# A planner of engine orders: TensorE priced by its recent columns, new overheads, less room at hand-overs

## What is computed

```python
x = x + 0.5 * ffn(layernorm(x))     # gate, up: 512 -> 1408 (ternary weights, scaled), silu(g) * u, down: 1408 -> 512
x = x + attn(layernorm(x))
x = x + 0.5 * ffn(layernorm(x))

def attn(x):                        # I = 1024 channels, N = 16 states, R = 128
    h, gate = split(x @ W_in.T)     # 512 -> 2 * 1024
    h = silu(causal_conv4(h) + conv_b)
    ts, B, C = split(h @ Wx.T, [128, 144]); each rms-normed
    delta = softplus(ts @ Wdt.T + dt_bias)
    # for each channel and each of 16 states, along the sequence:
    s = exp(delta * A) * s + delta * B * h
    y = sum_n s * C + D * h
    return (y * silu(gate)) @ Wout.T
```

## Time and profile before

| | before |
|---|---|
| median of 3 runs | 2842.37 us (2838.3 to 2843.48) |
| the profiled execution | 2835.58 us, span of its instructions 2833.8 us |
| PE busy | 2386.6 us, 84%, 12266 instructions |
| DVE busy | 2466.0 us, 87%, 3115 instructions |
| ACT busy | 1757.4 us, 62%, 2995 instructions |
| POOL busy | 2275.5 us, 80%, 1387 instructions |
| mean granted TensorE clock | 0.922 |
| DMA | 606.66 MB, 214 GB/s, 63.5% of the 16 engines' time |

### The profile page before, as it was taken

The page is one execution under the profiler, slowest core; times in us unless marked ns, Lnnn a source line. Parts: engine busy times, 40 slices in busy tenths (PEclk is TensorE's granted clock), DMA queues, the critical chain, the costliest instruction groups (busy, mean ns, idle before and its releaser), DMA issues. The chain is left out here.

```text
span 2833.8 us, 38163 instructions
## 1 busy us (share of the span) xinstructions
PE 2386.6 (84%) x12266; PEld 1933.5 (68%) x12266; DVE 2466.0 (87%) x3115; ACT 1757.4 (62%) x2995; POOL 2275.5 (80%) x1387
## 2 busy tenths in 40 slices
PE   6779789689577998889988999889988886599968
PEld 5657677577466776677766877677776764477756
DVE  5649997897998989899999999899989988999973
ACT  5465667767656666576657765577657666465531
POOL 2257769779976889789996999779996889889852
PEclk9889899899789999999999999999999997599979
DMA  8655645846666467955778366955778388366544
GB/s 268 225 191 167 238 160 178 297 131 230 205 214 235 127 211 265 310 172 172 248 267 314 129 216 237 322 202 166 235 266 283 121 287 289 101 206 188 183 165 141
DMA packets 293952, 606.66 MB, mean 214 GB/s; under 512 B 23024, under 2 KB 23792, under 8 KB 293744
## 3 DMA queue, kind: packets, MB, share of 16 engines
q1 hardware_dynamic: 293744, 604.13, 63.5%
HBM read 451.47 MB, written 152.57 MB: 213 GB/s over the span
## 5 line engine op out<-in xcount | busy, mean ns | idle before, releaser
L1930 POOL TENSOR_TENSOR sbuf<-dus,bring 128x1024 f32<-128x1024 f32 x512 | 1217.9, 2394 | 181.3 <-PE pt L1403 94.4
L1556 ACT ACTIVATE pa<-dls,cst 128x512 f32<-128x512 f32 x1024 | 691.8, 688 | 432.3 <-DVE sbuf L1730 415.8
L1403 PE MATMUL pt<-ident,sbuf 128*128 128x128 f32 x4096 | 645.0, 294 | 210.9 <-DVE sbuf L1730 84.1
L1403 PEld LDWEIGHTS pt<-ident,sbuf 128*128 128x128 f32 x4096 | 507.2, 150 | 367.4 <-DVE sbuf L1730 131.9
L1322 PE MATMUL pm<-xT,wring 128*128 128x512 f32 x2816 | 708.0, 399 | 16.1 <-DVE xT L1613 6.4
L1730 DVE TENSOR_TENSOR_SCAN sbuf<-pa,sbuf 128x512 f32<-128x512 f32 x512 | 610.0, 1211 | 64.6 <-ACT pa L1556 53.4
L1730 DVE TENSOR_TENSOR_SCAN sbuf<-pa,carry,sbuf 128x512 f32<-128x512 f32 x512 | 631.9, 1268 | 35.2 <-POOL sbuf L1930 23.1
L1334 PE MATMUL pm<-wring,act 128*128 128x512 f32 x2176 | 581.4, 410 | 25.1 <-DVE hd L1658 9.4
L1322 PEld LDWEIGHTS pm<-xT,wring 128*128 128x128 f32 x2816 | 516.6, 189 | 120.3 <-issue 18.4
L1741 DVE SCALAR_TENSOR_TENSOR acc<-pt,cT,acc 128x512 f32<-128x512 f32 x768 | 548.0, 739 | 51.6 <-PE pt L1403 49.9
L1334 PEld LDWEIGHTS pm<-wring,act 128*128 128x128 f32 x2176 | 401.6, 193 | 113.4 <-issue 14.4
(11 more groups left out here) (142 smaller groups left out, 2285.9 us busy)
## 6 DMA issues: line engine op xcount, KB each, us to landing
wring<-wsp SPq DMA_DIRECT2D x408, 512.0 KB, 4.5
bring<-b_d SPq DMA_DIRECT2D x256, 256.0 KB, 3.9
xn_d<-tb SPq DMA_DIRECT2D x24, 1024.0 KB, 9.1
xnb<-xn_d SPq DMA_DIRECT2D x19, 1024.0 KB, 7.3
x_d<-tb SPq DMA_DIRECT2D x16, 1024.0 KB, 6.1
u_d<-hd SPq DMA_DIRECT2D x64, 256.0 KB, 5.7
sg_d<-hd SPq DMA_DIRECT2D x64, 256.0 KB, 4.3
tb<-x_d SPq DMA_DIRECT2D x16, 1024.0 KB, 6.8
```

The costliest lines, as they stand in the source:

```text
L1403: ins = e.matmul(pt[u.pt[tt]][:, k * P:(k + 1) * P], sbuf[:, u.s3, k, tt * P:(tt + 1) * P], ident[:, :], is_transpose=True, start=True, st ...
L1556: e.activation(pa[k % 2][:, :], dls[:, k, :], ACT.Exp, scale=col(C_A + (4 * u.ig + k) * N + u.n)).then_inc(S.a_exp, 1)
L1930: e.tensor_tensor(sbuf[:, u.s3, h * m:(h + 1) * m, :], dus[:, h * m:(h + 1) * m, :], bring[:, u.s2:u.s2 + 1, :].broadcast_to([P, m, TC]), ...
```

## The change

Three things are changed, all in the planner. No instruction, tile, buffer or semaphore is added or removed; only the merged order of each engine's threads, SP's too, can come out differently, both in the first stage and in the rest.

1. PE is no longer priced with a fixed time. A matmul hands over its columns, and the new class `Columns` turns them into a duration: it divides planned time into slices from the plan's zero on, keeps count of the columns that each slice has seen, and lets work run at `FULL` (2270 columns per us) if the slice before counted at least `BUSY`, else at `HALF_RATE` (1200 columns per us). Nothing counts as less than 256 columns of time. A 512-column matmul costs 0.2256 us or 0.427 us, a transpose 0.113 us or 0.213 us.
2. DVE's fixed part is 0.064 instead of 0.05 us, and `LATE` changes by engine: PE 0.3 to 0.2, ACT 0.13 to 0.12, DVE 0.13 to 0.14, POOL 0.15 to 0.17.
3. `MARGIN` is 0.12 instead of 0.3 us. `SPARE` stays.

```diff
-MARGIN = 0.3
+MARGIN = 0.12
 DWELL = 12.0
+
+WINDOW, BUSY, FULL, HALF_RATE = 3.4133, 3060, 2270.0, 1200.0
 ISSUE, LAND = 0.42, 2.5
-LATE = {"pe": 0.3, "act": 0.13, "dve": 0.13, "pool": 0.15}
+LATE = {"pe": 0.2, "act": 0.12, "dve": 0.14, "pool": 0.17}
...
         self.events, self.time, self.up, self.table = [], 0.0, None, None
+        self.columns = ()
...
         elif self.eng == "dve":
-            self.time += 0.05 + n / 962.0 + more
+            self.time += 0.064 + n / 962.0 + more
...
     def matmul(self, out, a, b, is_transpose=False, **k):
         n = width(out)
-        self.time += 0.115 if is_transpose else 0.16 if n < 256 else n / 2140.0
+        self.columns += (max(256, n), 2 * n if is_transpose else n),
         return self
...
+class Columns:
+
+
+    def __init__(self):
+        self.count = {}
+
+    def run(self, t, work):
+        for n, counted in work:
+            left = 1.0
+            while left > 1e-9:
+                k = int(t / WINDOW + 1e-9)
+                whole = n / (FULL if self.count.get(k - 1, 0.0) >= BUSY else HALF_RATE)
+                part = min(left, ((k + 1) * WINDOW - t) / whole)
+                self.count[k] = self.count.get(k, 0.0) + part * counted
+                left -= part
+                t += part * whole
+        return t
...
         self.reach, self.now, self.clock, self.owner = {}, {}, {}, {}
+        self.columns = Columns()
...
-                end = at + s.time
+                end = self.columns.run(at, s.columns) if eng == "pe" else at + s.time
                 self.clock[eng] = end
                 end += LATE[eng]
```

## The result

| | before | after |
|---|---|---|
| median | 2840.34 us (4 runs) | 2872.93 us (2870.07 to 2874.39, 4 runs) |
| ratio after / before | | 1.0109, 95% interval 1.0088 to 1.0129 |
| span of the profiled execution | 2833.8 us | 2872.6 us |
| DVE busy | 2466.0 us | 2467.3 us |
| span less DVE busy | 367.8 us | 405.3 us |

What follows compares the result with a forecast made beforehand. DVE was taken as the bound, busy 2192.4 of 2400 us in the middle, leaving 207.6 us idle to win from. Gains 10 + 5 + 13 + 0 = 28 us gave 2842.4 - 28 = 2814 us, range 2785 to 2858.

Steps and rivals of the forecast that it cites:

- What bounds the kernel: Whole kernel: DVE is fullest; an order can win at most its 207.6 us of middle idle time; start and end stay.
- PE's price, 10 + 5 us: PE matmuls and transposes: clock-dependent prices gain 10 us at the lower clock and 5 us at the upper.
- the idle share at the lower clock: DVE in the middle: its 13% idle share there should come down towards the upper clock's 7.5%.
- Room and lateness, 13 us: Ring of ACT's exponential and DVE's recurrence: smaller room cuts a fifth of 64.2 us of waits, 13 us gained.
- Idle time from greedy choices that hold with any prices: Planner's merge: if the idle time comes from such choices, the prediction fails as a whole; no size given.
- DVE's overhead, 0 us: DVE's instructions: 14 ns more planned for each gains 0 us, with 10 us to either side.
- nothing to measure: a new draw from the same urn: Merged order: old waits vanish, others of the same sum appear; 2842 us, within 6; chance 0.12.
- The slower rival, late DMAs: Loads for POOL and PE: DMAs land later than planned, smaller room no longer hides it; 2867 us; chance 0.20 with other losses.
- not past 100: Waits for `bring`, `dus` and `wring`: growth past 100 us in all would show late DMAs at work.
- The rule of the skill: PE's clock: the gate's activity view is free-running and not reset at kernel start, while the plan sets slices from its zero.
- the 12 us at stake: PE's clock slices fall elsewhere than the chip's: gain 16 instead of 28 us, 2826 us; chance 0.21 jointly with POOL as bound.

Runs made afterwards that it cites:

- e1: The changed kernel with MARGIN put back to 0.3, all other new prices kept; ratio 1.0033 to the kernel before.
- e7: The changed kernel with MARGIN 0.13 instead of 0.12; ratio 1.0004 to the kernel before.
- e8: The changed kernel with MARGIN 0.11 instead of 0.12; ratio 1.0042 to the kernel before.
- e9: The changed kernel with LAND 2.8 instead of 2.5 us in the planner; ratio 1.0015 to the kernel before.
- e16: The changed kernel with MARGIN 0.13 and DMAs priced at 340 instead of 370 KB per us; ratio 1.0017 to the kernel before.
- e2: The kernel before with MARGIN 0.12 instead of 0.3 alone; ratio 1.0002 to the kernel before.
- e5: The kernel before with MARGIN 0.29 instead of 0.30; ratio 1.0076 to the kernel before.
- e6: The kernel before with MARGIN 0.31 instead of 0.30; ratio 1.0044 to the kernel before.
- e14: The kernel before with DMAs priced at 340 instead of 370 KB per us alone; ratio 1.0089 to the kernel before.
- e3: The kernel before with PE priced by Columns alone, MARGIN 0.3 and the old overheads kept; ratio 1.0045 to the kernel before.
- e4: The kernel before with the new LATE and DVE's 0.064 us alone; ratio 1.0076 to the kernel before.
- e18: The changed kernel with MARGIN 0.24 instead of 0.12, picked as a bad order by the replay; 2884.56 us, ratio 1.0154 to the kernel before.
- e11: The changed kernel's order with weight-piece loads after the first stage moving 64 of 128 partitions; 2882.11 us, ratio 1.0128 to the kernel before.

## Why the prediction was wrong

**What bounds the kernel** held. DVE's busy time is the same in all orders to 0.4%, the start stayed to about 2 us and the last two pieces of the closing chain to 0.02 us, and 32.7 of the 38.8 us are DVE's idle time in the middle.

**PE's price, 10 + 5 us.** The waits that the price bears on did shrink, by 10.8 us for the transposes, and that isn't the luck of one order: with all the new prices these waits are 33 to 43 us in the six orders that weren't picked (the changed kernel, e1, e7, e8, e9, e16; mean 37), with the old ones 48 to 75 in five (before, e2, e5, e6, e14; mean 57). But the gain didn't stay: the waits for the exponential average 75 us in those six and 65 in the five, and the mean ratios are 1.0037 and 1.0042. Which of the new prices does it isn't shown: e3 with the columns alone has 47.5 us of waits for the transposes, e4 with the overheads alone 61.0. In the changed kernel the idle share at the lower clock went from 13.4% to 11.9%, while that at the upper one rose from 7.5% to 9.2%, and the stretches at the lower clock grew from 358.4 to 471.1 us (sums of the windows at clock 0.50, then 1.00, of the changed kernel, as the earlier trace rows):

```profile
sum 471.05, PE 332.74 PEld 268.46 DVE 415.19 ACT 269.00 POOL 392.96; mean PE 6.16 PEld 4.97 DVE 7.69 ACT 4.98 POOL 7.28
...
sum 2047.99, PE 1819.68 PEld 1497.20 DVE 1860.58 ACT 1338.35 POOL 1752.71; mean PE 33.70 PEld 27.73 DVE 34.46 ACT 24.78 POOL 32.46
```

e3, with this part alone, measured +0.45% where I had -0.5%. That is within the scatter of e5 and e6 and so tells of no effect of its own.

**Room and lateness, 13 us.** This is the step that failed. The hand-overs fit the new room, as worked out from the earlier trace rows; but from "the plan is nearer to the trace" I went to "DVE waits less", and there is no such step. The waits for the exponential, of which I wanted a fifth gone, rose by 26.4 us. e2 shows the room alone at 1.0002, e18 shows twice the room at 1.0154. In the longest wait, long work was put ahead of the exponential on ACT, and that choice is a greedy one at any prices; that the other 107 waits are of this kind is not shown. Idle time from greedy choices that hold with any prices was the sign by which the prediction was to fail as a whole.

**DVE's overhead, 0 us**, with 10 to either side: e4 measured +0.76%, some 22 us, for it and `LATE` together; e5 measured as much for 10 ns of room, so neither zero nor a loss of its own is shown.

**The rivals.** The one nearest the truth was "nothing to measure: a new draw from the same urn". Its mechanism is what the runs showed, and its size was wrong: I gave the urn 6 us to either side. The twelve new orders that were not picked, the changed one, e1 to e9, e14 and e16, lie between 1.0002 and 1.0109, a width of 30 us. I also took the kernel before for a typical draw. None of the twelve is measured below it, so it was a good one, and any change that made a new order was likelier to lose. The means show no worth of the change itself: the new prices with 0.11, 0.12 and 0.13 average 1.0052, the old with 0.29, 0.30 and 0.31 average 1.0040. The slower rival, late DMAs, came out near in time, 2867 against 2872.9 us, by a sum that does not hold: the waits of POOL for `bring` and `dus` and of PE for `wring` together went from 67 to 79 us, not past 100, and halving the weight loads left the loss where it was. Its premise was misread besides: POOL's scan thread is in `SPARE` with 0, so POOL's product had no room behind B and `dus` in the old plan either, and `MARGIN` took none away; only PE's room behind `wring` shrank. That it was near in time is luck.

**The rule of the skill.** The Trainium skill (TensorE: Matmul & The Clock Gate, Part 1, "What's actually happening") warns against fitting a model to one count of matmuls at the lower clock. The runs can't tell whether the plan's slices missed the chip's, since the scatter of the orders is larger than the 12 us at stake.

**The range** should have held the scatter of single orders. Measured afterwards it is about 1% wide, and a forecast of this kind of change needs it on both sides.

**Still open** is which single choices make the changed kernel's order worse than its neighbours at 0.11 and 0.13, whether a slower price for DMAs is better on average, and what part of the spread is DMAs that land late in a crowd.

## What to carry to other kernels

When a kernel's order comes out of a greedy planner, run it also with a constant moved by an amount that can't matter; the change in time is the noise against which every edit of the planner must be read, and here it was 0.4 to 1.1%. A planner that is nearer to the trace isn't yet a better one: judge the finished order, and compare means over several neighbouring settings rather than one setting with another. Since orders can be had cheaply, it pays to make many and to pick one by replaying it with measured durations and somewhat longer DMAs, which gave 0.6 to 0.8% here in four picks of four, more than any price is shown to give.

## What was unexpected of the hardware

Halving a weight load from 512 to 256 KB, by leaving out 64 of its 128 partitions, took its median time to landing only from 4.5 to 3.8 us in the order of before and from 4.3 to 3.8 us in that of after. The kernel of before became 0.16% faster by it, and that of after no faster. Worked out from these medians as an estimate, the bytes of a whole load of this shape account for some 1.0 to 1.4 us of its 4.3 to 4.5. The shape counts as well, or the moment: the 15 weight loads of 256 KB over all 128 partitions landed in 3.0 us in the changed kernel, less than the halved ones.

```profile
wring<-wsp SPq DMA_DIRECT2D x15, 256.0 KB, 3.0
```

The median also hides a long tail. A load of B has a median of 3.7 us in e11 and took up to 14.2 us, and it is the slow ones that engines wait for: the eight loads that ended a wait of POOL had taken 5.4 to 14.2 us.
